# A LoRA and prompt-pooling kernel: one matmul padded to 128 rows, another to 128 weight columns

## The reference

```python
# layer 0: a low-rank term and an embedding, chosen by the row's language
t = einsum('bsd,brd->bsr', x, lora_A[lang])          # rank 16
x = x + einsum('bsr,bdr->bsd', t, lora_B[lang]) + lang_embed[lang][:, None, :]
# layer 1: masked softmax pooling, the mask chosen by the row's prompt type
scores = einsum('bsa,a->bs', tanh(x @ W1 + b1), v)   # 64 hidden units
mask = l <= j, l >= j or l != j                      # by prompt type
p = softmax(where(mask, scores[:, None, :], -1e30), axis=-1)
x = x + einsum('bjl,bld->bjd', p, x) / count(mask)
```

## Time and profile before

| | before |
|---|---|
| median of 2 runs | 150.32 us (150.1 to 150.55) |
| the profiled execution | 148.97 us, of which the span of the records is 147.0 |
| TensorE matmuls busy | 135.4 us, 92% |
| TensorE weight loads busy | 97.6 us, 66% |
| VectorE busy | 116.7 us, 79% |
| ScalarE busy | 99.8 us, 68% |
| POOL busy | 24.3 us, 17% |

### The profile page before, as it was taken

One profiled execution on the slowest core, in us unless ns is written; L12 is line 12 of the kernel. 1 busy time (PEld: TensorE's weight loads), 2 busy tenths in 40 slices (PEclk: granted clock), 3 DMA queues, 4 the chain that ended last, 5 costly groups with the idle time before them and its releaser, 6 DMA issues.

```text
span 147.0 us, 3608 instructions
## 1 busy us (share of the span) xinstructions
PE 135.4 (92%) x788; PEld 97.6 (66%) x789; DVE 116.7 (79%) x347; ACT 99.8 (68%) x233; POOL 24.3 (17%) x82
## 2 busy tenths in 40 slices
PE   5949999999999999999999889899999899999970
PEld 5827765666566566656656668677877777777750
DVE  5325688776675666667877899999999999999993
ACT  3104877666666766666675069998999799999900
POOL 7257632212112222212200000000000000000000
PEclk9996999999999999999999999999999999999997
DMA  3098005434443444342400000434444434444445
GB/s 55 8 305 267 3 4 145 143 84 132 141 116 105 141 139 119 101 141 77 142 0 0 4 0 2 143 136 155 144 145 147 150 140 170 172 152 147 143 148 208
DMA packets 19353, 17.18 MB, mean 117 GB/s; under 512 B 2886, under 2 KB 19338, under 8 KB 19338
## 3 DMA queue, kind: packets, MB, share of 16 engines
q1 hardware_dynamic: 19040, 16.95, 36.1%
q10 hardware_dynamic: 298, 0.07, 0.3%
HBM read 8.62 MB, written 8.39 MB: 116 GB/s over the span
## 4 chain that ended last, share of the span: by engine, by line
PE 67%; DVE 15%; issue 5%; DMA 5%; ACT 3%; SPq 2%; DVEq 1%; ACTq 0%
PE psum L354 19%; PE psum L341 13%; PE psum L468 10%; PE psum L366 9%; DVE yl L724 6%; PE psum L376 6%; DVE o L793 5%; DMA x_in<-in_x 5%; PE psum L449 3%; PE psum L382 3%; PE psum L453 2%; ACT yh L563 2%; ACT q L574 1%; DVE rz L788 1%; DVE zc L783 1%
## 5 line engine op out<-in xcount | busy, mean ns | idle before, releaser
L468 PE MATMUL psum<-yh,q 128*128 128x258 f32 x128 | 34.7, 303 | 2.1 <-DVE o L793 1.7
L354 PE MATMUL psum<-xT,wsel 128*112 128x256 f32 x128 | 33.6, 386 | 0.0
L468 PE MATMUL psum<-yl,q 128*128 128x258 f32 x128 | 32.1, 282 | 0.0
L724 DVE SCALAR_TENSOR_TENSOR yl<-x,g_col,yh 128x258 fp32r<-128x258 f32 x64 | 30.0, 478 | 0.4 <-ACT yh L563 0.2
L506 ACT COPY xT<-psum 128x512 f32<-128x512 f32 x32 | 18.7, 585 | 16.0 <-PE psum L341 15.7
L563 ACT ACTIVATE yh<-x,g_col 128x258 fp32r<-128x258 f32 (+1 forms) x64 | 29.4, 519 | 0.0
L574 ACT ACTIVATE q<-psum,q_bias 128x256 fp32r<-128x256 f32 x64 | 27.1, 480 | 3.0 <-PE psum L453 1.9
L468 PEld LDWEIGHTS psum<-yh,q 128*128 128x128 f32 x128 | 24.1, 189 | 6.5 <-issue 3.9
L793 DVE SCALAR_TENSOR_TENSOR o<-psum,rz,x 128x256 f32<-128x256 f32 x64 | 27.9, 480 | 0.1
L468 PEld LDWEIGHTS psum<-yl,q 128*128 128x128 f32 x128 | 24.2, 189 | 0.0
L341 PE MATMUL psum<-ident,x_in 128*128 128x128 f32 x128 | 21.3, 290 | 2.0 <-DMA x_in<-in_x 2.0
(11 more groups left out here) (98 smaller groups left out, 103.5 us busy)
## 6 DMA issues: line engine op xcount, KB each, us to landing
x_in<-in_x SPq DMA_DIRECT2D x32, 256.0 KB, 2.7
out<-o SPq DMA_DIRECT2D x31, 256.0 KB, 2.1
out<-o SPq DMA_DIRECT2D x2, 128.0 KB, 1.8
lB<-in_L_cond_lora_B SPq DMA_DIRECT2D x2, 32.0 KB
lAn<-in_L_cond_lora_A ACTq DMA_DIRECT2D x1, 64.0 KB
w<-in_L_cond_W SPq DMA_DIRECT2D x1, 64.0 KB
v_sb<-in_L_cond_v ACTq DMA_DIRECT2D x2, 0.2 KB, 3.5
ids_i<-in_itok_B SPq DMA_DIRECT2D x2, 16.0 KB
```

The lines of the kernel that those rows point to most:

```text
L354: last = nc.tensor.matmul(proj_ps[u % 2][0:M, 0:S], wsel[:, u % V, c, :], xT[:, u % 2, c, :], start=(c == 0), stop=(c == ND - 1))
L468: last = nc.tensor.matmul(pool_ps[u % 2][:, j, 0:DZ], q[:, u % V, s, j * P:(j + 1) * P], part_y[:, u % V, s, :], start=(s + k == 0), stop= ...
L724: ins = nc.vector.scalar_tensor_tensor(yl[:, u % V, s, :], of(x1[:, :, s, :], i, u).rearrange("p a d -> p (a d)"), of(g_col[:, s, :], i, u ...
```

## The change

The expansion contracts over all 128 partitions of tT and wselB and no longer over the 50 from 64 on. The rows of wselB outside those 50 are zero, and tT is filled with ones in all partitions at the start, so that what is added is zero times one. The score's weights v_row get 128 columns, of which the upper 96 are zero, and its output 128 partitions. What `select` copies into v_row for each pair of rows is still 32 columns. The number and order of the instructions on TensorE, ScalarE, VectorE and SP stay; POOL has one fill more at the start.

```diff
-        v_row = sb("v_row", [2 * A, V, B])
+        v_row = sb("v_row", [2 * A, V, P])
...
             nc.gpsimd.memset(low[:], 0.0)
+            nc.gpsimd.memset(v_row[:], 0.0)
             nc.gpsimd.memset(mask[:], 0.0)
...
-                    nc.gpsimd.tensor_copy(v_row[:, u // 2 % V, :], v_hot[:].rearrange("p k n -> p (k n)")[:, bass.ds(b * (B // 2), B)]
+                    nc.gpsimd.tensor_copy(v_row[:, u // 2 % V, 0:B], v_hot[:].rearrange("p k n -> p (k n)")[:, bass.ds(b * (B // 2), B)]
                                           ).then_inc(v_selected, 2)
...
-                    last = nc.tensor.matmul(lora_ps[u % 2][:, s * D:(s + 1) * D], tT[T0:K, u % V, s * P:(s + 1) * P],
-                                            wselB[T0:K, u % V, :], start=True, stop=True)
+                    last = nc.tensor.matmul(lora_ps[u % 2][:, s * D:(s + 1) * D], tT[:, u % V, s * P:(s + 1) * P],
+                                            wselB[:, u % V, :], start=True, stop=True)
...
-                nc.tensor.matmul(score_ps[0:B, 0:S], v_row[:, u // 2 % V, :], tanh[:, u // 2 % V, :],
+                nc.tensor.matmul(score_ps[:, 0:S], v_row[:, u // 2 % V, :], tanh[:, u // 2 % V, :],
                                  start=first, stop=final).then_inc(scored, 2)
...
-            nc.vector.memset(tT[T0:P, :, :].bitcast(fp32), 1.0)
+            nc.vector.memset(tT[:].bitcast(fp32), 1.0)
```

## The result

| | before | after |
|---|---|---|
| median of 2 runs | 150.32 us (150.1 to 150.55) | 141.81 us (141.56 to 142.05) |
| ratio to before | | 0.943, 95% interval 0.934 to 0.953 |
| the profiled execution | 148.97, span 147.03 | 141.56, span 139.87 |
| TensorE matmuls / loads busy | 135.4 / 97.6 us | 127.0 / 103.3 us |
| VectorE busy | 116.7 us, 79% | 117.6 us, 84% |

The kernel is 5.7% faster; 139.8 was forecast, with 137.0 to 143.5 as the range. I split the two profiled executions at three marks: low_t of row 0 (the start of VectorE's first row), n_row (the end of the first half), and the last VectorE instruction. All are starts or ends of records, in us.

A forecast was written before the change was run, and what follows sets the result against it. TensorE's row was taken to bound the first half: 11.2 us saved over 14 row pairs, less 0.5 and 0.3 for VectorE, makes 10.4. The profiled 148.97 becomes 138.6, or 139.8 on the median's footing; range 137.0 to 143.5.

The forecast's parts named there:

- TensorE's steps: First half: expansion 0.43 to 0.24, transposes 0.59 to 0.44, score 0.55 to 0.43; 14 row pairs save 11.2 us.
- The wider load at 0: Score weights of 128 columns: 16 scores pay between 0 and 1.8 us, taken as 0, since a matmul covers the load.
- Zeroing at 0: Larger fill of tT and new fill of v_row on POOL cost 0, the latter hidden by the wait for v.
- VectorE late at two places: VectorE falls behind in rows 2 to 7 (loss 0.3 us) and in rows 24 to 30 before n_row (loss 0.5).
- The tables' lateness: Rows 2 to 7: VectorE falls 0.7 behind, against about 0.9 of room at the expansion's wait; loss taken as 0.3 us.
- B: VectorE sets the first half's pace, register read bare, every row 1.90; gain 7.1 us, so 143.2; chance 0.12.
- C: Going between fp32 and fp32r breaks TensorE's stream even at full size; about 148.5 us; chance 0.07.
- D: The idle 0.09 goes, but no weight load starts beneath a matmul; some 5 us saved, 145.3; chance 0.04.
- F: Padding does nothing, something else makes the breaks and the wider load is bare; +0 to +1.8, 151.2 us; chance 0.03.
- E: TensorE's clock falls to 1.2 GHz at the seam of the halves; slower, over 2% above 150.3 us; chance 0.02.

The follow-up runs named there:

- e6: The changed kernel with the small type tables made at the start and all of pick moved to POOL; 138.12 us, ratio 0.917 to before.
- e3: The changed kernel with only the score padded to 128 columns, the expansion back at 50 rows; 148.15 us, ratio 0.989 to before.
- e1: The changed kernel run again with nothing edited; 141.55 us, ratio 0.944 to before.
- e4: The changed kernel with only the small type tables moved to the start, pick left on VectorE; 138.78 us, ratio 0.930 to before.

## Why the prediction was right, step by step

**TensorE's steps: right.** Transposes 0.44, expansion 0.24 (measured 0.23 to 0.24), score 0.43, rows of 1.54 and 1.97, pairs of 3.50: from 33.31 to 57.81 there are 14 rows in 24.50, which is 7 x 3.50. In e6, where nothing else holds TensorE back, the first expansion to n_row takes 11.7 less than before; the sum had 11.2 for its 14 pairs and counted nothing for the rows around them.

**The wider load at 0: right.** In the profile after it is under a matmul. e3 shows the 0.08 where it isn't. The 0.11 that the forecast read as a bare load, from 88.35 to 88.46, was not one, since a matmul starts in between:

```profile
88.38 0.36 PE L468 MATMUL psum<-yh,q 128*128 128x258 f32 x1
```

**Zeroing at 0: right for the fills themselves.** tT's fill takes 0.91 before and after, that of v_row 0.52 and ends ahead of POOL's wait for v, and v_hot starts 0.06 later. The start was late by TensorE's clock and the landing of x; whether the two halves together act on the clock stays open, as told with e1.

**VectorE late at two places: the places right, the sizes too small.** The sum had 0.3 at the start and 0.5 at the end, 0.8 in all. Measured against e6 it was 0.6 and 1.3, 1.9 in all: this is the term that was mis-sized, by 1.1 us. The tables' lateness was mostly met by the room before the expansion's wait for x1, as argued (0.2 to row 6), but it was carried to row 8 and cost 0.4 more there, at 31.19 in the chain. At the seam the argument gives e4's number, 0.64 for a forecast of 0.5; the changed kernel has 0.7 more. Of these, 0.36 could have been read in the trace of the kernel before: the forecast took its first row with pick from 70.60 to 72.69, but low_t of row 24 is at 66.24 there, the next at 68.75, so that the first row with pick already took 2.51, with the idle 0.70 at 67.37 shown under e4 (70.60 is row 26). The other 0.34 are the two picks of 0.59 beside POOL, which that trace does not have.

**The start and the end were not foreseen,** and the forecast lies near the median partly by luck. On the profiled executions, which the sum is made for, the gain was 7.2 us and not 10.4: VectorE's 1.1 too little, 1.6 at the end and 1.0 before the first expansion (19.34 for 18.33), less the 0.5 by which TensorE's gain was under-counted, are the 3.2 missing. Against the median of 141.81 only 2.0 are missing, since the profiled execution before lay 1.35 under its median and that after 0.25.

**The rivals.** B (1.90 a row, the read bare) failed: rows on TensorE's pace were 1.75 on average, with the read hidden in about every second one. C (a break from fp32 to fp32r) failed: 40.83 and 41.25 in the rows after have fp32 on either side of fp32r and no break. D (loads stay bare) failed: 40.80. The Trainium skill's sentence that loads overlap matmuls only with differing row groups (named with D in the prediction) does not hold for full-height matmuls here: two such, and the load lies beneath. The same section also allows it for a load into the background weight buffer, which D left out. F failed, since the breaks are gone and the kernel is 8.5 us faster. E didn't come, the clock stays up behind the seam: the half behind the seam took 63.03 for 63.05.

## What to carry to other kernels

Look for small matmuls, few rows or few weight columns, in a stream of larger ones: each passage in or out cost 0.12 to 0.20 us here (0.09 of standing and a bare weight load). Zeros that bring such a matmul up to 72 columns or 114 rows took the passage away and cost TensorE nothing, since the time of these matmuls went by the columns streamed; 64 columns were not enough. It takes both sides of every passage: padding the smaller offender alone gained 1%, the larger alone 5%. Then see what was hidden by the old pace, and move its odd jobs to where it waits. Here 1.9 us of an 11.7 us gain were lost to tables and pick, one-off work that stood in the paced rows. Moving it brought 2.4% more (138.1 us, ratio 0.917 to before), 1.9 us of it VectorE's and the rest at the kernel's end.

## What was not expected

- A matmul with 64 weight columns breaks the stream as one with 32 does, and one with 72 doesn't (score piece 0.58 and 0.43, transposes behind it 0.59 and 0.44).
- The last store's issue took 1.15 to 1.67 us instead of 0.45 in five of ten profiles, each with an instruction fetch at that moment: 1% of this kernel's time. What places the fetch is open.
- VectorE's pick took 0.59 to 0.63 instead of 0.42 where it began while POOL was copying wsel, 13 times of 13, and 0.42 where POOL's copy began after it. Its copy of wselB took up to 0.64 instead of 0.29 beside POOL's pick.
- The register read of row 24 left VectorE idle for 0.70 in eight profiles and for 0.34 in the two of kernels that make the tables at the start, though the edit touches neither that row nor that instruction.
- In the profile after, the granted clock reads 1.00 in a stretch in which matmuls run at half speed (four transposes over 1.11 us at 10.73; the kernel before has 1.11 too for those at 13.15, with a reading of 0.50). The record has no entry there before 14.37. The distance of the matmuls tells the clock where the record doesn't.
